# Results divided in one product and added by GpSimd, normalizations tile by tile, and scores for the maxima two a step: a decoder layer on one core

## The chip, the cores and the metric

The kernel runs on one core of a Trainium2 chip. The metric is the time of one execution on the device in microseconds (us), the median of several runs. The engines are TensorE (PE in the rows; PEld is its weight load), VectorE (DVE), ScalarE (ACT), GpSimd (POOL) and SyncE (SP), which issues most transfers. They run their own instruction streams in order and meet only at semaphores.

## The reference, cut to what matters

A decoder layer on x of 4 x 512 tokens by 512 features: causal self-attention, cross-attention to a context, and a mixture of experts, each behind a layer norm and added to x. The change lies in the cross-attention and in the layer norms computed beside it.

```python
x = x + attn(layernorm(x), w_qkv, w_proj)            # 16 heads of 128
x = x + xattn(layernorm(x), ctx_512, ctx_512)
x = x + ffn(layernorm(x), ...)                       # 8 experts, 2 a token, and a shared one

def xattn(q, k, v):      # 32 query heads, 8 key/value heads, D = 16, S = 512
    scores = einsum('bkgsd,bktd->bkgst', qh, kh) / 4
    weights = softmax(scores, axis=-1)
    out = einsum('bkgst,bktd->bkgsd', weights, vh)

def layernorm(x, eps=1e-5):
    return (x - mean(x)) / sqrt(var(x) + eps)
```

## The kernel before, in words

The residual x lies in SBUF all the time, in `res` (16 tiles of 128 tokens by 512). Self-attention runs to 954 us of the profile, cross-attention from there to 1462 us, the experts to the end.

Cross-attention works through 32 items, one for each batch b (0 to 3) and key/value head kv (0 to 7), and two more short rounds; item m is 8b + kv. Batch 0 and batch 3 are written out, batches 1 and 2 are two turns of one loop on every engine (`over_items`). In the program of an item, `cross_steps` lists what TensorE and the others do in eight steps. Three items overlap in it: the scores of the next item for its row maxima ("s", 16 a item, numbered S0 to S15 below, line 1084), the transposed scores of this item ("st", line 1095, followed by the exponential on ScalarE), the weights times the values of the last item ("pv", line 1106, in every odd step), and turns of 128 x 128 tiles on TensorE ("t", line 149): of keys ("k"), of queries ("q"), of queries with their maxima put in ("m"), and of the result of the item two before ("o", in step 4).

- VectorE takes the maximum of each score tile (line 1520). The scores use two banks of PSUM in turn, so score number u waits until the maximum of score u - 2 is taken (`s_xmax`, line 1083).
- When the turned result of an item is there, in step 4 behind S9, VectorE takes the reciprocals of the softmax sums (line 1595), multiplies the four tiles of the result by them in four products (line 1597), and adds the result to `res` (line 1603). The next turn on TensorE into the same bank waits for that add (`s_to`).
- GpSimd splits the normalized tokens `xn` into the queries of the item three ahead (`build_queries`, lines 778 to 783), adds up values (`build_values`), and puts the maxima into the queries, by pairs of heads (`put_maxima`, lines 790 to 797). TensorE's "m" turns wait for these. In item kv = 5 it first waits for all four tiles of the next batch's `xn`, then builds those queries, then the keys of the next batch (`build_keys`, lines 766 and 770), and only then puts in the first pair of maxima, for the "m" turn of step 6.
- The layer norm of the next batch is done at the start of an item, in one piece each, ahead of that item's maxima on VectorE: `moments` (four bn_stats, four bn_aggr, some small operations) at kv = 1, `roots` at kv = 2, `queries` (four products that write `xn`) at kv = 5. In batch 3, the moments for the experts' norm of batches 0 to 2 come at kv = 3, 4, 5, and the roots at kv = 4, 5, 6. The power between moments and roots is GpSimd's (line 735 or 839).

Of the kernel before, what the change touches and what calls it, by code (L numbers as in the profile page):

```python
# [6 lines left out]
P = 128  # L7
# [144 lines left out]
def moments(eng, count, src, st, first, n, s_var):  # L152

    tiles = slice(first, first + n)
    for t in range(n):
        ready = count.mark(eng.bn_stats(st["stats"][:, first + t, :], src[:, t, :]))  # L156
    eng.wait_ge(count.sem, ready)
# [20 lines left out]
RESULT_MARKS = 1 + TOK_TILES  # L178
# [8 lines left out]
VW = 32  # L187


def cross_steps(kv, m_left):  # L190
# [7 lines left out]
    for k in range(8):  # L198
        units = [("s", next(s_units)) for _ in range(1 if k % 2 else 3)] if m_left >= 1 else []
        if k % 2 == 0:  # L200
            ops += units[0:1]
            units = units[1:]
        if m_left >= 0:
            ops.append(("st", k))
        ops += units[0:1]
        if k in turns and (m_left >= turns[k][2] if turns[k][0] != "o" else kv >= 2):
            ops.append(("t",) + turns[k])
        ops += units[1:]
        if kv >= 1 and m_left >= -1 and k % 2:
            ops.append(("pv", k // 2))  # L210
    return ops


TA_START, TA_ITEM = 7, 5

# [152 lines left out]
def build(nc, x, ctx_in, w_qkv_t, w_proj_t, gate_t, w1_t, w2_t, w3_t, kinds, out):  # L368
# [11 lines left out]
    with ExitStack() as whole:  # L380
# [57 lines left out]
        s_ta = sem("s_ta")  # L438
        s_to = sem("s_to")
# [88 lines left out]
        xrec = sbb("xrec", [P, TOK_TILES, XG])  # L528
        xo = sbb("xo", [P, TOK_TILES, XG, XD])
# [187 lines left out]
        def _(pool):  # L717
# [90 lines left out]

            def cross(b, first, last):
                for kv in range(KV):  # L810
# [7 lines left out]
                    if kv == 1 and not last:  # L818
                        power_next(b)
# [26 lines left out]
            cross(BATCH - 1, False, True)  # L846

# [46 lines left out]
        def _(pe):  # L894
# [143 lines left out]
            def cross(b, kv, steps):  # L1038
# [7 lines left out]
                for op in steps:  # L1046
                    if op[0] == "t":
                        kind, which, off = op[1:]
                        if before_is_result:
                            pe.wait_ge(s_to, m - 1 if kind != "o" else m - 2)  # L1050
# [47 lines left out]
                    else:  # L1098
# [344 lines left out]
        def _(dve):  # L1443
# [66 lines left out]

            def queries(b):

                for t in range(TOK_TILES):
                    dve.tensor_scalar(xn[:, t, :], res_b[:, b, t, :], mv[:, t, 0:1], rstd[:, t:t + 1],
                                      ALU.subtract, ALU.mult).then_inc(s_xn2, 1)
# [53 lines left out]
            def cross(b, kv, steps):  # L1569
# [4 lines left out]
                if isinstance(b, int) and b == BATCH - 1:  # L1574

                    if 4 <= kv < 7:
                        roots(dve, count, norm, (kv - 4) * TOK_TILES, TOK_TILES, s_pow, 2 * BATCH + kv - 3)
                    if 3 <= kv < 6:
                        moments(dve, count, res_b[:, kv - 3], norm, (kv - 3) * TOK_TILES, TOK_TILES, s_var)
                if not (isinstance(b, int) and b >= BATCH - 1):  # L1580
                    if kv == 1:
                        moments(dve, count, res_b[:, b + 1], norm, 0, TOK_TILES, s_var)
                    if kv == 2:
                        roots(dve, count, norm, 0, TOK_TILES, s_pow, BATCH + 2 + b)
                    if kv == KV - 3:
                        dve.wait_ge(s_xq, KV * TOK_TILES * b + KV * TOK_TILES)
                        queries(b + 1)
                for op in steps:
                    if op[0] == "s":
                        maximum(m + 1, (kv + 1) % 2, op[1], XS)  # L1590
                    elif op[:2] == ("t", "o"):
# [236 lines left out]
```

## Time and profile before

| | us |
|---|---|
| median of 3 runs | 2003.03 (2002.97 to 2003.96) |
| profiled execution, its own time | 2004.67 |
| profiled execution, span in the trace | 2002.9 |
| TensorE busy in the span | 1867.5 (93%) |
| VectorE busy | 1087.9 (54%) |
| ScalarE busy | 970.2 (48%) |
| GpSimd busy | 262.9 (13%) |
| mean granted clock of TensorE | 0.971 of full speed |

Busy time of TensorE is modelled from the starts of pipelined matmuls; what counts in the rows is when a matmul starts and what it had waited for. A row of the timeline with `x4` merges four instructions that ran back to back, and its time covers all four.

### The profile page before, as it was taken

What the parts mean: (1) busy time and instruction counts of PE and PEld (TensorE: products, weight loads), DVE (VectorE), ACT (ScalarE), POOL (GpSimd) and SP (SyncE); (2) the same over time, 40 slices, a digit from 0 to 9 for tenths busy, and PEclk for the clock granted to TensorE, in tenths of its full rate; (3) what the DMA queues carried; (4) which work ended last, traced back from release to release, by engine and by line L of the source; (5) the groups of instructions that cost most, each with busy time, mean ns of one, the idle gap of its engine ahead of it and who ended that gap; (6) DMA issues with size and microseconds to landing.
All of it is one profiled execution on the core that took longest, in us unless ns stands there. A gap on an engine that the chain in (4) does not pass through costs nothing. (4 is left out here: it accounts for less than half of the span.)

```text
span 2002.9 us, 28767 instructions
## 1 busy us (share of the span) xinstructions
PE 1867.5 (93%) x9769; PEld 1316.1 (66%) x9769; DVE 1087.9 (54%) x2253; ACT 970.2 (48%) x1789; POOL 262.9 (13%) x751
## 2 busy tenths in 40 slices
PE   6999989998999989988899998998989599999998
PEld 5677667776677667765444443443379499999997
DVE  7433433342433433454777777778754126776756
ACT  3443434343433433333677776776742015666651
POOL 1000000000000000051242242433001400000015
PEclk9999989999899999999999998999989799999999
DMA  3000010000000000000000060000011318878756
GB/s 137 32 1 1 22 33 1 1 2 22 32 1 1 22 0 1 1 11 0 1 6 1 1 242 13 0 0 1 1 46 38 142 37 278 282 272 285 270 178 213
DMA packets 73393, 131.64 MB, mean 66 GB/s; under 512 B 4512, under 2 KB 35232, under 8 KB 73248
## 3 DMA queue, kind: packets, MB, share of 16 engines
q1 hardware_dynamic: 68128, 113.01, 16.4%
q0 software_dynamic: 5120, 16.78, 2.5%
q8 instruction: 80, 1.31, 0.3%
q14 instruction: 65, 0.53, 0.1%
HBM read 96.75 MB, written 33.03 MB: 65 GB/s over the span
## 5 line engine op out<-in xcount | busy, mean ns | idle before, releaser
L1520 DVE TENSOR_REDUCE xmax<-ps 128x1 f32<-128x512 f32 x512 | 329.2, 686 | 110.9 <-PE ps L1084 104.1
L1349 ACT ACTIVATE xp<-ps 128x1024 f32<-128x1024 f32 x256 | 262.9, 1029 | 140.1 <-PE ps L1095 136.2
L1282 ACT ACTIVATE probs<-ps,nmax 128x128 f32<-128x128 f32 (+3 forms) x256 | 135.5, 529 | 313.9 <-DVE nmax L1496 313.0
L1496 DVE TENSOR_REDUCE nmax<-ps 128x1 f32<-128x128 f32 (+3 forms) x256 | 126.2, 493 | 237.7 <-PE ps L926 232.1
L1084 PE MATMUL ps<-k,q 64*128 64x512 f32 x496 | 217.9, 479 | 34.3 <-DVE xmax L1520 34.3
L1084 PEld LDWEIGHTS ps<-k,q 64*128 64x128 f32 x496 | 86.0, 186 | 202.1 <-DVE xmax L1520 163.9
L926 PE MATMUL ps<-k_t,q_t 128*128 128x128 f32 (+3 forms) x512 | 201.1, 476 | 0.0
L1095 PE MATMUL ps<-q3m,k 64*128 64x512 f32 x512 | 181.9, 452 | 0.0
L149 PE MATMUL ps<-ident,probs 128*128 128x128 f32 x704 | 127.6, 286 | 42.1 <-DVE probs L1504 28.2
L1005 PE MATMUL ps<-pt,v_s 128*128 128x128 f32 (+3 forms) x512 | 161.0, 460 | 2.7 <-ACT pt L1320 2.5
L149 PEld LDWEIGHTS ps<-ident,probs 128*128 128x128 f32 x704 | 89.5, 145 | 100.6 <-issue 66.5
L1106 PE MATMUL ps<-xp,vx 128*32 128x512 f32 x1024 | 140.5, 623 | 1.4 <-issue 1.3
L143 PE MATMUL ps<-xh,wh 128*128 128x512 f32 x384 | 129.6, 459 | 2.1 <-DVE wl L1476 2.1
L143 PE MATMUL ps<-w12h,x_h 128*128 128x352 f32 x568 | 121.9, 336 | 10.0 <-issue 8.7
L1005 PEld LDWEIGHTS ps<-pt,v_s 128*128 128x128 f32 x512 | 88.4, 201 | 58.6 <-ACT pt L1320 32.4
L735 POOL TENSOR_TENSOR rstd<-ve,half 128x4 f32<-128x4 f32 x9 | 11.2, 1247 | 876.7 <-DVE ve L162 876.7
L1549 DVE TENSOR_TENSOR al<-ps,ah 128x512 fp32r<-128x512 f32 x64 | 44.3, 692 | 142.2 <-ACT ah L1325 142.2
L143 PE MATMUL ps<-w12h,x_l 128*128 128x352 f32 x568 | 115.9, 325 | 2.7 <-issue 1.8
L143 PE MATMUL ps<-w12l,x_h 128*128 128x352 f32 x568 | 115.1, 324 | 0.0
L1554 DVE TENSOR_TENSOR res<-ps,res 128x512 f32<-128x512 f32 x64 | 44.3, 692 | 123.2 <-PE ps L143 123.2
L1504 DVE TENSOR_SCALAR probs<-probs,rinv 128x128 f32<-128x128 f32 (+3 forms) x256 | 105.7, 413 | 9.1
L1320 ACT COPY pt<-ps 128x128 f32<-128x128 f32 (+3 forms) x256 | 108.8, 425 | 2.8 <-PE ps L149 2.7
(179 smaller groups left out, 3351.1 us busy)
## 6 DMA issues: line engine op xcount, KB each, us to landing
w_raw<-in_w_t SPq DMA_DIRECT2D x56, 704.0 KB, 5.9
w_raw<-in_w_t SPq DMA_DIRECT2D x28, 768.0 KB, 5.9
rows_x<-w_raw SPq DMA_DIRECT2D x1, 9984.0 KB, 30.0
mixed<-rows_x SPq DMA_DIRECT2D x39, 256.0 KB, 4.4
rows_y<-y_s SPq DMA_DIRECT2D x39, 256.0 KB, 5.4
w_raw<-in_w_qkv_t SPq DMA_DIRECT2D x4, 1536.0 KB, 6.6
res<-in_x SPq DMA_DIRECT2D x4, 1024.0 KB, 12.3
w_raw<-in_w_proj_t SPq DMA_DIRECT2D x4, 1024.0 KB, 5.1
```

Source lines behind the costliest of these rows:

```text
L143: last = pe.matmul(dst, lhs, rhs, start=(n == 0), stop=(n == len(pairs) - 1))
L149: return pe.matmul(dst, src, ident, start=True, stop=True, is_transpose=True)
L926: pe.matmul(ps[:, S_BANK + u % 2, 0:w], q_t[:, b % 2, h, i * P:w], k_t[:, b % 2, 0:w], start=False, stop=True, skip_group_check=True).then ...
L1005: ins = pe.matmul(ps[:, O_BANK + h % 2, j * P:], v_s[:, b % 2, j, :], pt[:, j, j * P:], start=(j == TOK_TILES - 1), stop=True, skip_group_ ...
L1084: pe.matmul(ps[:, XS + op[1] % 2, :], q3[half_of(h), (kv + 1) % 2, h // 2, i * P:(i + 1) * P], k3[half_of(h), (kv + 1) % 4, :], start=True ...
L1095: ins = pe.matmul(ps[:, XST + 2 * (t % 2) + h % 2, :], k3[half_of(h), kv % 4, t * P:(t + 1) * P], q3m[half_of(h), pair, :], start=True, st ...
L1106: ins = pe.matmul(ps[VW * h:VW * (h + 1), XO, :], vx[:, before % 4, j, :], xp[:, (kv - 1) % 2, h, j, :], start=(j == 0), stop=(j == TOK_TI ...
L1282: act.activation(probs[:, u % 4, 0:w], ps[:, S_BANK + u % 2, 0:w], ACT.Exp, bias=nmax[:, u % 4:u % 4 + 1], accum_out=rsum[:, u % 4:u % 4 + ...
L1320: act.copy(pt[:, 0:i + 1, i * P:(i + 1) * P], ps[:, T_BANK + (1 + t) % 2, 0:(i + 1) * P].rearrange("p (j n) -> p j n", n=P))\
L1349: act.activation(xp[:, kv % 2, 2 * pair:2 * pair + 2, t, :], ps[:, XST + 2 * (t % 2):XST + 2 * (t % 2) + 2, :], ACT.Exp, scale=X_SCALE).th ...
L1496: dve.tensor_reduce(nmax[:, u % 4:u % 4 + 1], ps[:, S_BANK + u % 2, 0:w], AX_X, ALU.max, negate=True).then_inc(s_max, 1)
L1520: dve.tensor_reduce(xmax[:, slot, i, h:h + 1], ps[:, bank + u % 2, :], AX_X, ALU.max, negate=True).then_inc(s_xmax, 1)
```

## The change

The result takes one product of 128 x 256 in place of four of 128 x 64 (`divide`), and writes it to one of two buffers; GpSimd then adds it to `res` (`add_result`), between the two `put_maxima` of the item. TensorE's next turn into the bank waits for the product (`s_od`) and not for the add. The product is made at the end of the step, or behind the next maximum.

Moments, roots and queries are cut up and placed behind steps ("end" in the list, `norm_piece`): one bn_stats behind steps 1, 3, 5 and 7 of item kv = 1, what gathers them behind step 0 of kv = 2, the roots behind step 0 of kv = 4, and the four tiles of `xn` behind steps 5 and 7 of kv = 4 and steps 0 and 1 of kv = 5. In batch 3 the same pieces come at kv = 2 to 4 (stats), 3 to 5 (gathered) and 5 to 7 (roots). Each step has two scores, where even steps had three and odd steps one.

```diff
@@ cross_steps @@
-        units = [("s", next(s_units)) for _ in range(1 if k % 2 else 3)] if m_left >= 1 else []
-        if k % 2 == 0:
-            ops += units[0:1]
-            units = units[1:]
+        units = [("s", next(s_units)) for _ in range(2)] if m_left >= 1 else []
+        ops += units[0:1]
         if m_left >= 0:
             ops.append(("st", k))
-        ops += units[0:1]
+        ops += units[1:]
         if k in turns and (m_left >= turns[k][2] if turns[k][0] != "o" else kv >= 2):
             ops.append(("t",) + turns[k])
-        ops += units[1:]
         if kv >= 1 and m_left >= -1 and k % 2:
             ops.append(("pv", k // 2))
+        ops.append(("end", k))
...
+QUERY_AT = [(4, 5), (4, 7), (5, 0), (5, 1)]
@@ GpSimd @@
+            def add_result(b, kv, m):
+                pool.wait_ge(s_od, m - 1)
+                at = ((kv - 2) % KV) * XG * XD
+                dst = res[:, :, :].rearrange("p (b t) c -> p b t c", b=BATCH)[:, b - (kv < 2), :, at:at + XG * XD]
+                pool.tensor_tensor(dst, xo[:, kv % 2].rearrange("p (t h) d -> p t (h d)", t=TOK_TILES), dst, ALU.add)\
+                    .then_inc(s_to, 1)
...
-                    if kv == 1 and not last:
+                    if kv == 3 and not last:
                         power_next(b)
...
-                    if last and 3 <= kv < 6:
-                        power(kv - 3, 2 * BATCH + kv - 2)
+                    if last and 4 <= kv < 7:
+                        power(kv - 4, 2 * BATCH + kv - 3)
                     if not (last and kv == KV - 1):
                         put_maxima((kv + 1) % 4, 0, 16 * m + 24, 2 * m + 3)
+                    if not (first and kv < 2):
+                        add_result(b, kv, m)
+                    if not (last and kv == KV - 1):
                         put_maxima((kv + 1) % 4, 1, 16 * m + 32, 2 * m + 4)
@@ TensorE @@
-                            pe.wait_ge(s_to, m - 1 if kind != "o" else m - 2)
+                            pe.wait_ge(s_od, m - 1 if kind != "o" else m - 2)
@@ VectorE @@
+                def norm_piece(k):
+                    if isinstance(b, int) and b == BATCH:
+                        return
+                    if final:
+                        if 2 <= kv < 5 and k % 2:
+                            if k == 1:
+                                dve.wait_ge(s_to, KV * (kv - 1))
+                            tile_moments(dve, count, res_b[:, kv - 2], norm, (kv - 2) * TOK_TILES, k // 2)
+                        if 3 <= kv < 6 and k == 0:
+                            gather_moments(dve, count, norm, (kv - 3) * TOK_TILES, TOK_TILES, s_var)
+                        if 5 <= kv and k == 0:
+                            roots(dve, count, norm, (kv - 5) * TOK_TILES, TOK_TILES, s_pow, 2 * BATCH + kv - 4)
+                        return
+                    if kv == 1 and k % 2:
+                        tile_moments(dve, count, res_b[:, b + 1], norm, 0, k // 2)
+                    if (kv, k) == (2, 0):
+                        gather_moments(dve, count, norm, 0, TOK_TILES, s_var)
+                    if (kv, k) == (4, 0):
+                        roots(dve, count, norm, 0, TOK_TILES, s_pow, BATCH + 2 + b)
+                    if (kv, k) in QUERY_AT:
+                        t = QUERY_AT.index((kv, k))
+                        if t == 0:
+                            dve.wait_ge(s_xq, KV * TOK_TILES * b + KV * TOK_TILES)
+                        query(b + 1, t)
+                def divide(ready):
+                    dve.wait_ge(s_dve, ready)
+                    if not (isinstance(m, int) and m < 4):
+                        dve.wait_ge(s_to, m - 3)
+                    o = ps[:, XT, :].rearrange("p (g d) -> p g d", d=VW)
+                    dve.tensor_tensor(xo[:, kv % 2], o[:, :, 0:XD],
+                                      xrec[:, :].unsqueeze(2).to_broadcast([P, TOK_TILES * XG, XD]), ALU.mult)\
+                        .then_inc(s_od, 1)
                 for op in steps:
                     if op[0] == "s":
                         maximum(m + 1, (kv + 1) % 2, op[1], XS)
+                    if op[0] in ("s", "end") and pending is not None:
+                        divide(pending)
+                        pending = None
+                    if op[0] == "end":
+                        norm_piece(op[1])
+                    if op[:2] == ("t", "o"):
                         dve.wait_ge(s_ot, m - 1)
-                        o = ps[:, XT, :].rearrange("p (t h d) -> p t h d", t=TOK_TILES, h=XG)
-                        count.seal(dve, dve.reciprocal(xrec[:, :, :], o[:, :, :, XD]))
-                        for t in range(TOK_TILES):
-                            ready = count.mark(dve.tensor_tensor(
-                                xo[:, t], o[:, t, :, 0:XD],
-                                xrec[:, t, :].unsqueeze(2).to_broadcast([P, XG, XD]), ALU.mult))
-                        dve.wait_ge(s_dve, ready)
-                        at = ((kv - 2) % KV) * XG * XD
-                        dst = res_b[:, b - (kv < 2), :, at:at + XG * XD]
-                        dve.tensor_tensor(dst, xo[:, :, :, :].rearrange("p t h d -> p t (h d)"), dst, ALU.add)\
-                            .then_inc(s_to, 1)
+                        o = ps[:, XT, :].rearrange("p (g d) -> p g d", d=VW)
+                        pending = count.mark(dve.reciprocal(xrec[:, :], o[:, :, XD]))
```

On VectorE, from the end of item 3 to item 5 of batch 0, there stands before (xmax is a maximum of a score tile, xrec the reciprocals, xo the divided result, xn a tile of normalized tokens):

```order
L1520 TENSOR_REDUCE xmax<-ps 128x1 x16
L1595 RECIPROCAL xrec<-ps 128x16
L1597 TENSOR_TENSOR xo<-ps,xrec 128x64 x4
L1603 TENSOR_TENSOR res<-xo,res 128x4x64
L1520 TENSOR_REDUCE xmax<-ps 128x1 x6
L1514 TENSOR_SCALAR xn<-res,mv,rstd 128x512 x4
L1520 TENSOR_REDUCE xmax<-ps 128x1 x10
L1595 RECIPROCAL xrec<-ps 128x16
L1597 TENSOR_TENSOR xo<-ps,xrec 128x64 x4
L1603 TENSOR_TENSOR res<-xo,res 128x4x64
```

and at the same place of the changed kernel:

```order
L1654 RECIPROCAL xrec<-ps 128x16
L1639 TENSOR_TENSOR xo<-ps,xrec 128x256
L1548 TENSOR_REDUCE xmax<-ps 128x1 x2
L1537 TENSOR_SCALAR xn<-res,mv,rstd 128x512
L1548 TENSOR_REDUCE xmax<-ps 128x1 x4
L1537 TENSOR_SCALAR xn<-res,mv,rstd 128x512
L1548 TENSOR_REDUCE xmax<-ps 128x1 x2
L1537 TENSOR_SCALAR xn<-res,mv,rstd 128x512
L1548 TENSOR_REDUCE xmax<-ps 128x1 x2
L1537 TENSOR_SCALAR xn<-res,mv,rstd 128x512
L1548 TENSOR_REDUCE xmax<-ps 128x1 x6
L1654 RECIPROCAL xrec<-ps 128x16
```

The add has left VectorE, the product is one, and the fourth tile of xn now stands behind the fourth maximum of item 5, where all four stood ahead of its first.

Also on VectorE, the moments in item 1, before (all of item 0's and item 1's maxima around one block):

```order
L1520 TENSOR_REDUCE xmax<-ps 128x1 x16
L156 BN_STATS stats<-res 128x6 x4
L158 MEMSET nt 128x4
L160 BN_AGGR mv<-stats 128x2 x4
L162 TENSOR_SCALAR ve<-mv 128x4
L1520 TENSOR_REDUCE xmax<-ps 128x1 x16
```

and now (the first row has the 16 maxima of item 0 and four of item 1):

```order
L1548 TENSOR_REDUCE xmax<-ps 128x1 x20
L160 BN_STATS stats<-res 128x6
L1548 TENSOR_REDUCE xmax<-ps 128x1 x4
L160 BN_STATS stats<-res 128x6
L1548 TENSOR_REDUCE xmax<-ps 128x1 x4
L160 BN_STATS stats<-res 128x6
L1548 TENSOR_REDUCE xmax<-ps 128x1 x4
L160 BN_STATS stats<-res 128x6
L1548 TENSOR_REDUCE xmax<-ps 128x1 x2
L167 MEMSET nt 128x4
L169 BN_AGGR mv<-stats 128x2 x4
L171 TENSOR_SCALAR ve<-mv 128x4
```

Each bn_stats stands behind four maxima, and the rest of the block behind two more.

On GpSimd, item 5 of batch 0, behind the queries (vx is build_values, kc build_keys, xq<-xmax put_maxima), before:

```order
L787 TENSOR_TENSOR vx<-kc 128x4x16 [waits s_xpv]
L766 TENSOR_TENSOR kc<-ctx_s,ones 128x16x16 [waits s_ctx,s_vx,s_kt]
L766 TENSOR_TENSOR kc<-ctx_s,ones 128x16x16 x7
L770 TENSOR_TENSOR kc<-ctx_s,kc 128x16x16 [waits s_pc]
L770 TENSOR_TENSOR kc<-ctx_s,kc 128x16x16 x3
L756 TENSOR_TENSOR xq<-xmax,ones 128x4x2 [waits s_xmax]
L796 TENSOR_TENSOR xq<-xmax,xq 128x4x2 [waits s_pm]
L756 TENSOR_TENSOR xq<-xmax,ones 128x4x2 [waits s_xmax]
L796 TENSOR_TENSOR xq<-xmax,xq 128x4x2 [waits s_pm]
```

and now:

```order
L798 TENSOR_TENSOR vx<-kc 128x4x16 [waits s_xpv]
L777 TENSOR_TENSOR kc<-ctx_s,ones 128x16x16 [waits s_ctx,s_vx,s_kt]
L777 TENSOR_TENSOR kc<-ctx_s,ones 128x16x16 x7
L781 TENSOR_TENSOR kc<-ctx_s,kc 128x16x16 [waits s_pc]
L781 TENSOR_TENSOR kc<-ctx_s,kc 128x16x16 x3
L767 TENSOR_TENSOR xq<-xmax,ones 128x4x2 [waits s_xmax]
L807 TENSOR_TENSOR xq<-xmax,xq 128x4x2 [waits s_pm]
L826 TENSOR_TENSOR res<-xo,res 128x4x64 [waits s_od]
L767 TENSOR_TENSOR xq<-xmax,ones 128x4x2 [waits s_xmax]
L807 TENSOR_TENSOR xq<-xmax,xq 128x4x2 [waits s_pm]
```

Only the add of the result has come in. TensorE's whole list of instructions is the same in both kernels, row by row, since a step of three scores and one of one, laid end to end, give the same order as two steps of two.

## Rows read from the trace of the kernel before

**Rows 1.** The page's first line: span and instructions.

```profile
span 2002.9 us, 28767 instructions
```

**Rows 2.** Waits, 950 to 1465 us: engine, line, waited for, us, times, longest.

```profile
PEld ps L1084 <- DVE xmax L1520: 163.9, 299, 3.3
```

**Rows 3.** Timeline of TensorE, item 25: start, us, what, idle before.

```profile
1356.44 1.06 PE L1106 MATMUL ps<-xp,vx 128*32 128x512 f32 x8
1357.88 0.49 PE L1084 MATMUL ps<-k,q 64*128 64x512 f32 x1 [0.38 <-DVE xmax L1520]
...
1358.91 0.65 PE L149 MATMUL ps<-ident,xq 128*128 128x128 f32 x4
```

**Rows 4.** Timeline of VectorE, items 25 to 27.

```profile
1354.66 1.29 DVE L1520 TENSOR_REDUCE xmax<-ps 128x1 f32<-128x512 f32 x2 [0.73 <-PE ps L1084]
1355.87 0.25 DVE L1595 RECIPROCAL xrec<-ps 128x16 f32<-128x16 f32 x1
1356.15 0.62 DVE L1597 TENSOR_TENSOR xo<-ps,xrec 128x64 f32<-128x64 f32 x4
1356.80 0.43 DVE L1603 TENSOR_TENSOR res<-xo,res 128x256 f32<-128x256 f32 x1
1357.15 2.56 DVE L1520 TENSOR_REDUCE xmax<-ps 128x1 f32<-128x512 f32 x4
...
1362.36 2.56 DVE L1520 TENSOR_REDUCE xmax<-ps 128x1 f32<-128x512 f32 x4 [1.04 <-PE ps L1084]
1366.27 2.57 DVE L1520 TENSOR_REDUCE xmax<-ps 128x1 f32<-128x512 f32 x4 [1.35 <-PE ps L1084]
...
1376.14 2.46 DVE L156 BATCH_NORM_STATS2 stats<-res 128x6 f32<-128x512 f32 x4
```

**Rows 5.** Timeline of ScalarE: the copy that closes items 16 to 18.

```profile
1221.88 0.59 ACT L1357 COPY o_t<-ps 128x512 f32<-128x512 f32 x1 [0.19 <-PE ps L1106]
...
1240.21 0.59 ACT L1357 COPY o_t<-ps 128x512 f32<-128x512 f32 x1 [0.20 <-PE ps L1106]
...
1255.30 0.59 ACT L1357 COPY o_t<-ps 128x512 f32<-128x512 f32 x1 [0.19 <-PE ps L1106]
```

**Rows 6.** The same copy, closing items 25 to 29.

```profile
1361.96 0.59 ACT L1357 COPY o_t<-ps 128x512 f32<-128x512 f32 x1 [0.19 <-PE ps L1106]
...
1376.87 0.59 ACT L1357 COPY o_t<-ps 128x512 f32<-128x512 f32 x1 [0.19 <-PE ps L1106]
...
1393.68 0.59 ACT L1357 COPY o_t<-ps 128x512 f32<-128x512 f32 x1 [0.20 <-PE ps L1106]
...
1412.53 0.59 ACT L1357 COPY o_t<-ps 128x512 f32<-128x512 f32 x1 [0.19 <-PE ps L1106]
...
1431.38 0.59 ACT L1357 COPY o_t<-ps 128x512 f32<-128x512 f32 x1 [0.19 <-PE ps L1106]
```

**Rows 7.** Timeline of TensorE: first scores of items 1 and 2.

```profile
966.11 0.46 PE L1084 MATMUL ps<-k,q 64*128 64x512 f32 x1
...
985.33 0.49 PE L1084 MATMUL ps<-k,q 64*128 64x512 f32 x1
```

**Rows 8.** Windows, item 17: us, busy time of each engine, then the granted clock.

```profile
1226.00:1228.00 2.00, 2.00 (x9) 0.92 (x12) 0.93 (x2) 1.56 (x2) 0.40 (x2) 0.50 0.00 0
```

**Rows 9.** Timelines of VectorE, TensorE and GpSimd, item 21.

```profile
1284.76 1.91 DVE L1514 TENSOR_SCALAR xn<-res,mv,rstd 128x512 f32 x4
...
1285.34 0.50 PE L1084 MATMUL ps<-k,q 64*128 64x512 f32 x1
...
1286.83 2.05 POOL L756 TENSOR_TENSOR xq<-xn,ones 128x64 fp32r<-128x64 f32 x8 [1.00 <-DVE xn L1514]
...
1295.41 3.00 POOL L770 TENSOR_TENSOR kc<-ctx_s,kc 128x256 fp32r<-128x256 f32 x4
...
1298.65 0.22 POOL L796 TENSOR_TENSOR xq<-xmax,xq 128x8 fp32r<-128x8 f32 x1
...
1298.92 0.66 PE L149 MATMUL ps<-ident,xq 128*128 128x128 f32 x4 [0.73 <-POOL xq L796]
```

More of the change, by code:

```diff
@@ L152, in moments, with tile_moments, gather_moments @@
 def moments(eng, count, src, st, first, n, s_var):
+    for t in range(n):
+        tile_moments(eng, count, src, st, first, t)
+    gather_moments(eng, count, st, first, n, s_var)
+def tile_moments(eng, count, src, st, first, t):
+    count.mark(eng.bn_stats(st["stats"][:, first + t, :], src[:, t, :]))
+def gather_moments(eng, count, st, first, n, s_var):
     tiles = slice(first, first + n)
-    for t in range(n):
-        ready = count.mark(eng.bn_stats(st["stats"][:, first + t, :], src[:, t, :]))
-    eng.wait_ge(count.sem, ready)
+    eng.wait_ge(count.sem, count.start + count.n)
     count.mark(eng.memset(st["nt"][:, tiles], 0.0))
@@ L176 @@
 NORM_MARKS = 2 * TOK_TILES + 5
-RESULT_MARKS = 1 + TOK_TILES
+RESULT_MARKS = 1
 KV, XG, XD = 8, 4, 16
@@ L438, in build @@
         s_ta = sem("s_ta")
+        s_od = sem("s_od")
         s_to = sem("s_to")
@@ L527, in build @@
         xmax = sbb("xmax", [P, 2, TOK_TILES, XG])
-        xrec = sbb("xrec", [P, TOK_TILES, XG])
-        xo = sbb("xo", [P, TOK_TILES, XG, XD])
+        xrec = sbb("xrec", [P, TOK_TILES * XG])
+        xo = sbb("xo", [P, 2, TOK_TILES * XG, XD])
         pb.close()
@@ L846, in _ @@
             cross(BATCH - 1, False, True)
+            for kv in range(2):
+                add_result(BATCH, kv, KV * BATCH + kv)
             pool.wait_ge(s_to, ITEMS)
@@ L1097, in cross @@
                         ins.then_inc(s_st, 1)
-                    else:
+                    elif op[0] == "pv":
                         j, before = op[1], (kv - 1) % KV
@@ L1509, in _, with query @@
             res_b = res[:, :, :].rearrange("p (b t) c -> p b t c", b=BATCH)
+            def query(b, t):
+                dve.tensor_scalar(xn[:, t, :], res_b[:, b, t, :], mv[:, t, 0:1], rstd[:, t:t + 1],
+                                  ALU.subtract, ALU.mult).then_inc(s_xn2, 1)
             def queries(b):
                 for t in range(TOK_TILES):
-                    dve.tensor_scalar(xn[:, t, :], res_b[:, b, t, :], mv[:, t, 0:1], rstd[:, t:t + 1],
-                                      ALU.subtract, ALU.mult).then_inc(s_xn2, 1)
+                    query(b, t)
             def maximum(m, slot, u, bank):
@@ L1573, in cross @@
                 count = counts[-1]
[L1574 to L1583, printed above, removed]
-                        roots(dve, count, norm, 0, TOK_TILES, s_pow, BATCH + 2 + b)
-                    if kv == KV - 3:
-                        dve.wait_ge(s_xq, KV * TOK_TILES * b + KV * TOK_TILES)
-                        queries(b + 1)
+                final = isinstance(b, int) and b == BATCH - 1
@@ L1590, in cross @@
                         maximum(m + 1, (kv + 1) % 2, op[1], XS)
[L1591 to L1604 removed]
+                    if op[0] in ("s", "end") and pending is not None:
+                        divide(pending)
+                        pending = None
+                    if op[0] == "end":
+                        norm_piece(op[1])
+                    if op[:2] == ("t", "o"):
+                        dve.wait_ge(s_ot, m - 1)
+                        o = ps[:, XT, :].rearrange("p (g d) -> p g d", d=VW)
+                        pending = count.mark(dve.reciprocal(xrec[:, :], o[:, :, XD]))
             over_items(cross)(dve)
```

## The prediction, made before the changed kernel ran

> **What bounds the kernel now.** I read the page first. The change touches only cross-attention, so I asked for the waits of that stretch. Neither TensorE nor VectorE fills it: TensorE's scores wait for VectorE's maxima, 163.9 us in 299 waits [rows 2], and the maxima wait for scores in between. So the stretch is a ping-pong over two banks, and what counts is where VectorE does something else while TensorE wants a bank. The reader is to see three places of that kind in the timelines.
>
> First, the result, in nearly every item. The reciprocal starts at 1355.87, the maximum that TensorE needs next at 1357.15, so VectorE is away for 1.28 us [rows 4]. TensorE's product with the values ends at 1357.50 (1356.44 + 1.06), it stands for 0.38 us until the next score at 1357.88, the score behind that is late too, and the turn starts at 1358.91 [rows 3]. An ordinary item lasts 14.91 us in written-out code (1361.96 to 1376.87) [rows 6] and 15.09 us in the loop (1240.21 to 1255.30) [rows 5].
>
> Second, the blocks of the layer norm. Item 27 begins with four bn_stats of 2.46 us together and their small operations [rows 4] and lasts 16.81 us, 1.90 over the ordinary; items 28 and 29, with moments and roots in one block, last 18.85 us each, 3.94 over [rows 6]. Item 17 has the moments alone and lasts 18.33 us, 3.24 over [rows 5], since TensorE's granted clock was 0.50 there, which is 1.2 GHz where 2.4 is full [rows 8]: it fell after TensorE had stood waiting for the block. Against the 1.90 of item 27 the clock cost 1.34 us. Item 1 lasts from 966.11 to 985.33, 19.22 us [rows 7]; it has no result to divide, so I take 14.4 for it without the block (14.91 less the 0.5 or so that the result costs), and it is 4.8 over.
>
> Third, GpSimd in items 5, 13 and 21. In item 21 it starts the queries at 1286.83, when the fourth tile of xn has ended (1284.76 + 1.91 = 1286.67), works without a break through queries, values and keys, and puts in the first maxima at 1298.65; TensorE's turn follows at 1298.92 after standing 0.73 us [rows 9]. GpSimd is already the last one there.
>
> **The change part by part.** The order of TensorE's instructions is the same, so "two a step" by itself is worth nothing; it only names the places behind which VectorE's pieces go.
>
> The result: reciprocal 0.28 us start to start (1355.87 to 1356.15), then one product of 256 elements a partition. No row has that product. The add of the same 256 elements took 0.43, and 0.35 start to start (1356.80 to 1357.15); the four products took 0.62 [rows 4]. I take the 0.35, since it has the same number of elements in one instruction, with the 0.62 as the upper end and the 0.25 that the reciprocals of 16 elements took as the lower. The next maximum then starts 0.28 + 0.03 + 0.35 = 0.66 us after the reciprocal, not 1.28, a gain of 0.62; the loop has one more wait with a computed value, so I take 0.60 for all. Does TensorE get it? The next score had 0.38 us to gain and the one behind it waits for the second maximum, so that and the turn move by all 0.6. The ends are 0.35 (product 0.62) and 0.7 (product 0.25). Items that have it whole: 2, 3, 6, 7, 8, 10, 11, 14, 15, 16, 18, 19, 22, 23, 24, 25. 16 x 0.60 = **9.6 us**.
>
> The moments: a bn_stats costs 2.46/4 = 0.61 us. Behind steps 1, 3 and 7 VectorE stands idle 1.35, 0.73 and 1.04 us for the next score [rows 4], which covers it; if that cover went, each would cost up to 0.61. Behind step 5 there is no idle time, and it takes just what the shorter result gave, so items 9, 17, 26, 27 and 28 gain nothing from the result. Gathering and roots stand behind the second maximum, where TensorE needs the third only after a product with values; up to about 1 us hides. So the blocks' prices come back: items 1, 9, 17, 27, 28, 29: 4.8 + 1.9 + 3.24 + 1.90 + 3.94 + 3.94 = **19.7 us**, with item 9 taken like item 27.
>
> Small change: in items 4, 12 and 20 a tile of xn (1.91/4 = 0.48 us [rows 9]) stands behind step 5, leaving 0.12 of the 0.60 each; in items 29 and 30 the roots with what stands beside them are longer than what hides them, I keep 0.3 of the 0.60 in each. Together **1.0 us**.
>
> The queries, which is the part against: all four tiles of xn stood ahead of the item's first maximum, and now the last stands behind its fourth. In item 21 GpSimd started 1.49 us after the item's first score (1285.34 to 1286.83) [rows 9]. Now: the score takes 0.50, two maxima 1.28 (2.56/4 each [rows 4]), a tile 0.48, two maxima 1.28, the last tile 0.48, and 0.16 to hand over as before, 4.18 us. GpSimd starts 2.7 us later, nothing on it is shorter (the add stands behind the maxima it is late with), and it was already late. TensorE reaches its turn earlier and stands there: the turn was 13.58 us into the item (1298.92 - 1285.34), is at 16.3, and without the wait would be at about 11.6. So the three items get 3 x 2.7 = 8.1 us longer, and TensorE stands some 4 us in each. After such a stand the clock fell in item 17; I add its 1.34 us in two of the three, since the rows don't show a fall behind every stand (item 27 had the same block as item 17 and kept its clock, by its length). **-10.8 us**. Two queues pass on this delay: behind GpSimd's first maxima stand the add, the second maxima and the next queries, but the second maxima wait for S15 anyway, so nothing more is late.
>
> GpSimd's add: the nearest row is L770, two inputs from SBUF and 128 x 256, 3.00/4 = 0.75 us [rows 9], against 0.43 on VectorE. It stands between the two pairs of maxima, and the second pair waits for S15, over 6 us behind the result, so the add is hidden there. The Trainium skill (GPSIMD Engine Reference, section 3, Performance versus the Vector engine) says elementwise work is about twice as slow on GpSimd and gives "use DVE for elementwise" as the rule; the rows agree on the ratio. The add is waited for once, the last one before the experts: 0.75 - 0.43 and a hand-over, **-0.35 us**.
>
> Sum: 9.6 + 19.7 + 1.0 - 10.8 - 0.35 = 19.2 us. The profiled span of 2002.9 [rows 1] lies within 0.2 of the median 2003.03 (that execution's own time was 2004.67), so I set the sum against the median: **1984 us**.
>
> **The rivals.**
> - GpSimd is in time after all (the wait for xn is not what starts it, or the turn finds the maxima ready). Then the -10.8 goes and the three items gain up to 0.6 each as well: 2003 - 31 = 1972 to 1973. Against it: the row of 0.73 us shows GpSimd late already. 1 in 10.
> - The product costs what the four did, or the stands in items 5, 13 and 21 cost twice the clock price because they are twice as long as item 17's: 16 x 0.25 = 4 us, or 3 x 1.34 = 4 us less gain. 1988. Nothing in the rows excludes either. 15 in 100.
> - The shorter result doesn't reach TensorE, because the second of the two scores waits for something else there (the copies of ScalarE, the turn's bank): 9.6 and 1 go; or VectorE and TensorE do wait for GpSimd's slower add in every item, 30 x (0.75 - 0.43) = 9.6. 1994 to 1995. The timeline names the maximum as the one waited for, and the only wait for the add, before a product, is for that of four items before, so 11 in 100. The second half of this is what the rule of the Trainium skill quoted above (GPSIMD Engine Reference, section 3) would lead one to expect.
> - Slower: TensorE's clock. The clock fell after stands of TensorE; if the new rhythm, with VectorE's pieces spread over many items, made it fall in ordinary items too, each fall would cost 1.34 us. The 19.2 us are used up after 14 falls, and it is slower by over 0.2% from 18 on. The rows show ordinary items, with stands of 0.4 us, at even length, and the spreading takes stands away. 4 in 100.
>
> **How the numbers follow.** The forecast has 60 in 100. The range of 8 in 10 goes from 1973, the first rival, to 1993: the ends of the product's price (0.35 to 0.7 us on 16 items, +4 and -2), the clock price (0 to 2 x 1.34 in three items, +5 and -3) lie inside. 0.2% is 4 us, about what a measurement of this kernel tells from no change: below 1999 is faster. All cases but the last and a part of the third lie there: faster 0.93, same 0.04, slower 0.03.
>
> **What would show it.** In the profile of the changed kernel: ordinary items 14.3 us written out and 14.5 in the loop; one product of some 0.4 us and the next maximum 0.66 us after the reciprocal; items 1, 27, 28 and 29 near 14.4 to 15, with no fall of the clock there; items 13 and 21 at 19 to 21 us, longer than before, with TensorE waiting over 4 us for GpSimd's put_maxima, and a granted clock near 0.5 behind it; GpSimd's add 0.75 us, waited for by nobody but the end. The prediction is wrong if that wait is not there, or if the ordinary items keep their length.

## The result, and the profile after

The changed kernel takes **1986.07 us** (median of 6 runs, 1977.9 to 1991.96), the kernel before 2003.49 us (median of 6, 2001.99 to 2008.4) in the same comparison: a ratio of 0.9906, 95% interval 0.9881 to 0.993. That is 17.4 us, with 19.2 forecast: faster, and inside the range. The profiled execution of the changed kernel is its slowest run (1991.96 us).

The first line of the page, which answers to [rows 1]:

```profile
span 1990.0 us, 28687 instructions
```

The waits of the stretch, which answer to [rows 2] (engine, line, waited for, us in total, times, longest): one more line of the kernel before (950 to 1465 us), then the changed kernel (950 to 1450 us):

```profile
PE ps L1084 <- DVE xmax L1520: 34.3, 44, 3.0
```

```profile
PEld ps L1109 <- DVE xmax L1548: 137.8, 330, 3.5
...
PE ps L149 <- POOL xq L807: 13.4, 3, 4.5
POOL xq L767 <- DVE xn L1537: 12.1, 3, 4.1
...
PE ps L1109 <- DVE xmax L1548: 5.1, 6, 3.2
```

The wait for the maxima fell from 163.9 to 137.8 us ahead of TensorE's weight loads, and from 34.3 us in 44 waits to 5.1 in 6 ahead of its matmuls. Between the two stands a pair of three waits each, and these are items 5, 13 and 21: GpSimd waits 12.1 us for the layer-normed tiles, and TensorE 13.4 us for GpSimd. That is the part of the prediction that spoke against the change.

VectorE and then TensorE around the result of an ordinary item (24), which answer to [rows 4] and [rows 3] (start, us, what, idle before and who ended it):

```profile
1346.98 0.25 DVE L1654 RECIPROCAL xrec<-ps 128x16 f32<-128x16 f32 x1
1347.26 0.42 DVE L1639 TENSOR_TENSOR xo<-ps,xrec 128x256 f32<-128x256 f32 x1
1347.60 1.28 DVE L1548 TENSOR_REDUCE xmax<-ps 128x1 f32<-128x512 f32 x2
```

```profile
1347.55 1.06 PE L1131 MATMUL ps<-xp,vx 128*32 128x512 f32 x8
...
1348.55 0.49 PE L1109 MATMUL ps<-k,q 64*128 64x512 f32 x1
...
1349.36 0.66 PE L149 MATMUL ps<-ident,xq 128*128 128x128 f32 x4
```

From the reciprocal to the next maximum it is 0.62 us (1346.98 to 1347.60) where it was 1.28, and one product takes 0.42. The score behind the product with values has no wait any more (it had 0.38 us), and the turn starts 1.81 us after that product's start (1347.55 to 1349.36), where it was 2.47.

ScalarE's copy closes each item, so the spacing of these rows is the length of an item. Items 1 and 2, then 4 and 5, then 20 and 21, then 27 to 29; they answer to [rows 5] and [rows 6]:

```profile
981.03 0.59 ACT L1382 COPY o_t<-ps 128x512 f32<-128x512 f32 x1 [0.37 <-PE ps L1131]
995.44 0.58 ACT L1382 COPY o_t<-ps 128x512 f32<-128x512 f32 x1 [0.36 <-PE ps L1131]
...
1024.44 0.58 ACT L1382 COPY o_t<-ps 128x512 f32<-128x512 f32 x1 [0.44 <-PE ps L1131]
1045.12 0.58 ACT L1382 COPY o_t<-ps 128x512 f32<-128x512 f32 x1 [1.07 <-PE ps L1131]
...
1274.48 0.58 ACT L1382 COPY o_t<-ps 128x512 f32<-128x512 f32 x1 [0.44 <-PE ps L1131]
1294.75 0.59 ACT L1382 COPY o_t<-ps 128x512 f32<-128x512 f32 x1 [0.62 <-PE ps L1131]
...
1382.01 0.59 ACT L1382 COPY o_t<-ps 128x512 f32<-128x512 f32 x1 [0.44 <-PE ps L1131]
1396.72 0.58 ACT L1382 COPY o_t<-ps 128x512 f32<-128x512 f32 x1 [0.44 <-PE ps L1131]
1411.14 0.59 ACT L1382 COPY o_t<-ps 128x512 f32<-128x512 f32 x1 [0.35 <-PE ps L1131]
```

Item 2 lasts 14.41 us and item 29 14.42: an ordinary item in written-out code was 14.91. Item 9 lasts 14.88, item 28 14.71 (it was 18.85), item 5 20.68 and item 21 20.27 (before: 17.83 and 16.50). The last copy of all comes at 1438.39, and came at 1459.17 before: cross-attention ends 20.8 us earlier. It also began 0.35 us later (its first score at 955.24, 954.89 before), so the stretch itself is 21.1 us shorter.

GpSimd and TensorE in item 21, which answer to [rows 9]:

```profile
1278.43 2.04 POOL L767 TENSOR_TENSOR xq<-xn,ones 128x64 fp32r<-128x64 f32 x8 [4.05 <-DVE xn L1537]
...
1290.01 0.22 POOL L807 TENSOR_TENSOR xq<-xmax,xq 128x8 fp32r<-128x8 f32 x1
1290.18 0.73 POOL L826 TENSOR_TENSOR res<-xo,res 128x256 f32 x1
```

```profile
1274.34 0.49 PE L1109 MATMUL ps<-k,q 64*128 64x512 f32 x1
...
1290.29 1.02 PE L149 MATMUL ps<-ident,xq 128*128 128x128 f32 x4 [4.46 <-POOL xq L807]
```

GpSimd starts 4.09 us into the item (1274.34 to 1278.43, was 1.49) and then works without a break up to its maxima at 1290.01; TensorE stands 4.46 us for them. Windows from within that stand to behind it (us, then busy time of PE, PEld, DVE, ACT and POOL, the granted clock, DMA):

```profile
1288.00:1290.00 2.00, 0.00 (x0) 0.00 (x0) 0.00 (x0) 0.00 (x0) 1.94 (x4) 1.00 0.00 0
1290.00:1292.00 2.00, 1.72 (x8) 1.12 (x8) 0.00 (x0) 0.58 (x1) 0.90 (x2) 0.61 0.00 0
1292.00:1294.00 2.00, 2.00 (x12) 0.92 (x12) 1.29 (x2) 1.48 (x2) 0.49 (x3) 0.54 0.00 0
```

In the first window only GpSimd works. After it TensorE comes back at a granted clock of 0.61 and 0.54, near its lower level of 1.2 GHz, and the four transposes of the turn take 1.02 us, not 0.66. In item 17, where [rows 8] showed 0.50 before, the clock is now full:

```profile
1226.00:1228.00 2.00, 1.99 (x16) 0.90 (x8) 2.00 (x5) 1.01 (x2) 0.57 (x1) 1.00 0.00 0
```

Last, the profiled span is only 12.9 us shorter (2002.9 to 1990.0), 7.9 less than cross-attention gained. TensorE's last transposes of fn start at 1971.96 in the kernel before and at 1953.43 after, so 18.5 us were left then; between cross-attention and that point 2.3 had gone, which I didn't follow to one wait. The other 5.6 us went in the last three expert steps. First the kernel before, then the changed one, TensorE:

```profile
1978.65 0.91 PE L143 MATMUL ps<-w12h,x_h 128*128 128x352 f32 x4 [1.05 <-DVE x_l L1618]
1979.40 0.80 PE L143 MATMUL ps<-w12l,x_h 128*128 128x352 f32 x4
...
1998.08 0.85 PE L1223 MATMUL ps<-w3h,hl 128*128 128x512 f32 x3
```

```profile
1957.00 0.32 PE L143 MATMUL ps<-w12h,x_l 128*128 128x352 f32 x1 [0.83 <-issue]
...
1964.44 1.54 PE L143 MATMUL ps<-w12h,x_h 128*128 128x352 f32 x4 [2.28 <-DVE x_l L1668]
1965.78 1.38 PE L143 MATMUL ps<-w12l,x_h 128*128 128x352 f32 x4
...
1985.15 0.87 PE L1248 MATMUL ps<-w3h,hl 128*128 128x512 f32 x3
```

The lead is 18.5 us at the transposes, 14.2 at the first pair (1978.65 to 1964.44) and 12.9 at the end. In between TensorE stood with nothing that the profile shows (0.83), waited 2.28 us where it had waited 1.05, and then ran its products at 1.38 us for four, not 0.80. The diff touches nothing there. Whether it belongs to the change or to one execution, the profile can't say; the sixth experiment answers it.

### The profile page after: what moved, and what is told of

The parts are those of the page before. It is cut to its first block and busy times, and to the rows that moved or that the text cites. A ratio compares the mean times of both kernels' runs of the same rounds, so it can differ in the third digit from the quotient of the medians.

```text
span 1990.0 us, 28687 instructions
## 1 busy us (share of the span) xinstructions
PE 1869.1 (94%) x9769; PEld 1321.3 (66%) x9769; DVE 1066.1 (54%) x2125; ACT 966.2 (49%) x1789; POOL 283.9 (14%) x783
## 5 line engine op out<-in xcount | busy, mean ns | idle before, releaser
L1109 PEld LDWEIGHTS ps<-k,q 64*128 64x128 f32 x496 | 85.5, 185 | 170.9 <-DVE xmax L1548 137.8
```

What stands on the lines that cost most here:

```text
L1109: pe.matmul(ps[:, XS + op[1] % 2, :], q3[half_of(h), (kv + 1) % 2, h // 2, i * P:(i + 1) * P], k3[half_of(h), (kv + 1) % 4, :], start=True ...
```

## The experiments

Experiments 1 to 4 ran in one comparison on one chip, 5 to 7 in another on another. The kernel before took 1972.85 us there (1971.81 to 1975.54, 10 runs) and 1974.08 (1971.58 to 1976.37, 9 runs), so only differences within a comparison are read.

**1. The queries earlier.** All four tiles of xn go behind odd steps of item 4 (12, 20), so GpSimd has them when it comes.

```diff
-QUERY_AT = [(4, 5), (4, 7), (5, 0), (5, 1)]
+QUERY_AT = [(4, 1), (4, 3), (4, 5), (4, 7)]
```

> The changed kernel with the four tiles of xn behind steps 1, 3, 5 and 7 of item kv = 4 in place of steps 5, 7 of kv = 4 and 0, 1 of kv = 5. Theory (the late fourth tile is what starts GpSimd late in items 5, 13 and 21): GpSimd starts the queries within 0.3 us of the item's first score in place of 4.1, its first maxima are put in 4 us earlier, TensorE waits for them 0.3 to 0.8 us in place of 4.5, the clock does not fall there, and the three items last about 15.1 us in place of 20.3 to 20.9: some 16 us less than the changed kernel, about 1968 us. Rival (GpSimd is late because its keys take 7.7 us whenever it starts, or because of something other than xn): the three items stay above 18 us and the time within 5 us of the changed kernel's 1985.

Measured: 1935.2 us (1934.97 to 1936.72), ratio 0.981 [0.9797, 0.9824], 37.6 us under the kernel before. Items 5, 13 and 21 last 14.74, 14.78 and 14.77 us. GpSimd, then TensorE:

```profile
1260.89 2.05 POOL L767 TENSOR_TENSOR xq<-xn,ones 128x64 fp32r<-128x64 f32 x8
```

```profile
1272.75 0.66 PE L149 MATMUL ps<-ident,xq 128*128 128x128 f32 x4 [0.37 <-POOL xq L807]
```

GpSimd waits for nothing ahead of the queries, and TensorE stands 0.37 us, not 4.46; the four transposes take 0.66 us again. The three items take 44.29 us together, 17.6 less than in the first profile of the changed kernel (61.88), and this kernel's gain is 17.4 us over the one that experiment 6 finds for the changed kernel (37.6 less 20.2). So the late last tiles of xn are the cause of the long items, and the clock's price goes with the stand. Against the items of experiment 6 (63.04 us) it is 18.8 less, and item 16, at the loop's end, takes 1.8 of it back here (20.11 us against 18.30; last section).

**2. The same, and GpSimd's keys in two halves.** The first maxima stand between the halves of build_keys, so GpSimd's chain ahead of them is shorter by the 2.8 us of the second.

```diff
 # GpSimd, item 5, 13, 21; the QUERY_AT of experiment 1
-                        build_keys(b + 1)
+                        build_keys(b + 1, (0,))
...
                         put_maxima((kv + 1) % 4, 0, 16 * m + 24, 2 * m + 3)
+                    if kv == KV - 3 and not last:
+                        build_keys(b + 1, (1,))
```

> As e1, and GpSimd puts in the first pair of maxima between the two halves of build_keys (after the eight products, before the four subtractions). Theory: GpSimd's first maxima are ready before TensorE's turn, no wait is left in items 5, 13 and 21, they last 14.4 to 14.6 us; another 1 to 2 us less than e1, about 1966.5 us. Rival (the next item's turn of keys now waits for the second half): the waits move by one item and e2 is no faster than e1, or slower by up to 2 us.

Measured: 1932.4 us (1930.98 to 1935.05), ratio 0.9794 [0.978, 0.9807]: the fastest kernel of the study, 40.4 us under the kernel before, where the changed kernel is 20.2 (experiment 6). Items 5, 13 and 21 last 14.44, 14.50 and 14.51 us, like any other, and no turn of maxima waits for GpSimd. The three items give 0.84 us of the 2.8 by which it is faster than experiment 1, and in the profiles item 16 is 1.22 shorter (18.89 and 20.11); the intervals of the two kernels overlap, so only the first part is shown to come from the edit. The turn of keys in the next item, which the rival had wait, doesn't: items 6, 14 and 22 last 14.41 to 14.51 us.

**3. The result part alone.** One product and GpSimd's add as in the change, the blocks of the layer norm where they were before.

```diff
-                    if kv == 1 and k % 2:
-                        tile_moments(dve, count, res_b[:, b + 1], norm, 0, k // 2)
...
+                    if kv == 1:
+                        moments(dve, count, res_b[:, b + 1], norm, 0, TOK_TILES, s_var)
```

> The result part alone: one product, add by GpSimd, norm blocks at the start of items as before. Theory: every item with a result but 5, 13 and 21 is 0.5 to 0.6 us shorter than before, 26 of them, and the blocks cost what they did: 13 to 16 us faster than before, 1988 us. Rival (the shorter result only pays where a piece of the norm takes its place, or GpSimd's add slows its maxima): under 5 us faster.

Measured: 1958.29 us (1954.22 to 1959.77), ratio 0.9926 [0.9913, 0.994], 14.6 us. Ordinary items last 14.42 and 14.50 us as in the changed kernel. The block still costs, but less than it did: item 28 lasts 17.04 us, 2.62 over the ordinary, where the excess was 3.94. VectorE at the start of item 28:

```profile
1376.86 0.15 DVE L179 TENSOR_TENSOR nt<-rstd 128x4 f32<-128x4 f32 x1
...
1377.82 2.47 DVE L160 BATCH_NORM_STATS2 stats<-res 128x6 f32<-128x512 f32 x4
...
1380.82 2.56 DVE L1548 TENSOR_REDUCE xmax<-ps 128x1 f32<-128x512 f32 x4
```

VectorE is away from TensorE's maxima for 3.96 us (1376.86 to 1380.82), and it was away for as long before, 3.94 (1392.95 to 1396.89). What differs is TensorE's granted clock behind the block. A window that begins some 3 us after the block's end, in the kernel before, then in this one:

```profile
1400.00:1402.00 2.00, 2.00 (x12) 0.51 (x4) 0.15 (x1) 0.00 (x0) 0.00 (x0) 0.50 0.04 8
```

```profile
1384.00:1386.00 2.00, 2.00 (x15) 1.01 (x11) 1.31 (x3) 1.06 (x2) 0.00 (x0) 1.00 0.03 8
```

So 1.3 us of the 3.94 were the clock (18.85 - 17.04, less 0.49 for the result), as in item 17. Behind the six blocks it fell in items 1, 17, 28 and 29 in the profile before and in items 1, 9 and 17 in this one. How long TensorE had stood doesn't decide it alone: here the clock fell after stands of 1.80 and 1.81 us (items 9 and 17) and stayed full after 2.61 and 2.49 (items 28 and 29). Item 9 is longer here than before (17.80 against 16.93), since the clock had stayed full there before.

**4. The norm part alone.** The pieces behind the steps as in the change; four products and VectorE's add as before.

```diff
-                    dve.tensor_tensor(xo[:, kv % 2], o[:, :, 0:XD],
-                                      xrec[:, :].unsqueeze(2).to_broadcast([P, TOK_TILES * XG, XD]), ALU.mult)\
-                        .then_inc(s_od, 1)
+                    for t in range(TOK_TILES):
+                        ready = count.mark(dve.tensor_tensor(x4[:, t], o[:, t, :, 0:XD],
+                                                             r[:, t, :].unsqueeze(2).to_broadcast([P, XG, XD]), ALU.mult))
+                    dve.wait_ge(s_dve, ready)
...
+                    dve.tensor_tensor(dst, xo[:, kv % 2].rearrange("p (t h) d -> p t (h d)", t=TOK_TILES), dst, ALU.add)\
```

> The norm part alone: pieces behind steps as in the changed kernel, the result in four products and an add on VectorE as before. Theory: the blocks give back 19.7 us, items 5, 13 and 21 lose about 11, and the pieces behind step 5, which now find no room, cost 0.5 each in eight items, 4 us: about 5 us faster than before, 1998 us. Together with e3 that makes the whole change (-15 and -5). Rival (the parts help each other, the sum is not the whole): e4 slower than before.

Measured: 1964.57 us (1964.28 to 1970.73), ratio 0.9963 [0.995, 0.9975], 8.3 us. Items 28 and 29 last 15.37 and 14.91 us, items 5, 13 and 21 21.11, 21.07 and 21.25. So the pieces gain at the blocks and lose at the queries, with the result as it was, and each piece behind step 5 costs what was expected (15.37 against 14.91). Some 5 us were expected, and 4.0 of the 8.3 are item 16 alone, 16.02 us where it was 20.02: a stand at the loop's end was shorter in this kernel (last section). Leaving item 16 out (it gained 0.5 in experiment 3 and 1.7 in experiment 6), the parts gave 14.1 and 4.3 us, 18.4 together, and the whole change 18.5: they add up. Item 16 is read from one execution of each kernel and the 95% intervals of the gains are 2.5 to 3 us to either side, so this is additivity within a few microseconds.

**5. One product, the add on VectorE.** The changed kernel with the add back on VectorE behind the product.

```diff
-                    if not (first and kv < 2):
-                        add_result(b, kv, m)
...
+                    dve.wait_ge(s_dve, ready)
...
+                    dve.tensor_tensor(dst, xo[:, kv % 2].rearrange("p (t h) d -> p t (h d)", t=TOK_TILES), dst, ALU.add)\
+                        .then_inc(s_to, 1)
```

> The changed kernel with the add on VectorE behind the one product, not on GpSimd. Theory (of the 0.63 us an item that VectorE gives back, the one product is 0.28 and the missing add 0.35): the next maximum starts 0.28 later than in the changed kernel at least, 1.00 us behind the reciprocal in place of 0.62; ordinary items last 14.8 us in place of 14.4 to 14.5, the whole 8 to 9 us more than e6. Rival (moving the add is worth nothing since VectorE has room): equal to e6 within 2 us.

Measured: 1963.34 us (1959.02 to 1963.61), ratio 0.9941 [0.9927, 0.9954], 9.4 us over the changed kernel in the same comparison. Ordinary items last 14.72 and 14.90 us. VectorE:

```profile
1368.11 0.25 DVE L1652 RECIPROCAL xrec<-ps 128x16 f32<-128x16 f32 x1
1368.40 0.42 DVE L1632 TENSOR_TENSOR xo<-ps,xrec 128x256 f32<-128x256 f32 x1
1368.86 0.42 DVE L1638 TENSOR_TENSOR res<-xo,res 128x256 f32<-128x256 f32 x1
1369.20 1.28 DVE L1544 TENSOR_REDUCE xmax<-ps 128x1 f32<-128x512 f32 x2
```

The next maximum starts 1.09 us after the reciprocal: 0.62 with the add on GpSimd, 1.28 in the kernel before. So of the 0.66 us that the result part takes from VectorE, 0.47 come from moving the add and 0.19 from the one product; of the item's 0.49 us in written-out code 0.30 and 0.19.

**6. The changed kernel again.** The same code as the change, in the later comparison (so no edit to show).

> The changed kernel once more, beside the kernels of this call. Theory: the 16.6 us between it and e1 and the sum of e3 and e4 hold on this chip: 1.0% to 1.2% faster than before, 19 to 23 us; cross-attention ends 20 to 21 us earlier than before, with items 5, 13 and 21 at 20 to 21 us. What differs from run to run lies behind cross-attention: the gathers and scatters of the experts. Rival (cross-attention itself varies): its items differ from the first profile by more than 2 us in all.

Measured: 1953.93 us (1950.6 to 1958.58), ratio 0.9898 [0.9882, 0.9913], 20.2 us under the kernel before. Its items 5, 13 and 21 last 20.92, 21.06 and 21.06 us. In its last three expert steps the four products take 0.80 to 0.89 us and none takes 1.38, so the loss there in the first profile doesn't come with the change each time. The expectation on cross-attention was missed, and its rival came about: the last closing copy comes at 1441.57, 17.6 us earlier than in the kernel before (whose only profile is of the first comparison) and not 20 to 21. Of the 3.2 us against the first profile, 2.2 lie ahead of the first closing copy, in item 0 and the start of item 1, where the granted clock is 0.50 from 963 to 970 us:

```profile
964.00:966.00 2.00, 2.00 (x10) 1.23 (x9) 1.29 (x2) 1.29 (x2) 0.00 (x0) 0.50 0.00 0
```

TensorE had stood for no more than 0.40 us at a time since 955. Experiments 2 and 7 show a fall at the same place, the first profiles and the other experiments don't; what brings it isn't shown. The remaining 1 us is mostly the clock behind the stands of items 5, 13 and 21, which reached into items 6 and 14 here (14.90 and 14.83 us), less 0.8 at item 16.

**7. The last tile of xn later still.** One step more.

```diff
-QUERY_AT = [(4, 5), (4, 7), (5, 0), (5, 1)]
+QUERY_AT = [(4, 5), (4, 7), (5, 0), (5, 2)]
```

> The changed kernel with the fourth tile of xn behind step 2 of item kv = 5 in place of step 1. Theory (every microsecond that the last tile is later makes the item as much longer): GpSimd starts 2.2 to 2.4 us later, TensorE stands 6.7 us in place of 4.5, items 5, 13 and 21 last 22.5 to 23.2 us, about 7 us more than e6 in all. Rival (the stand is set by the clock or by the keys): under 3 us more.

Measured: 1959.91 us (1957.78 to 1963.04), ratio 0.9927 [0.9914, 0.9941], 6.0 us over the changed kernel. Items 5, 13 and 21 last 22.40, 23.40 and 23.39 us. GpSimd, then TensorE, in item 21:

```profile
1287.02 2.05 POOL L767 TENSOR_TENSOR xq<-xn,ones 128x64 fp32r<-128x64 f32 x8 [6.40 <-DVE xn L1537]
```

```profile
1298.87 1.12 PE L149 MATMUL ps<-ident,xq 128*128 128x128 f32 x4 [6.80 <-POOL xq L807]
```

GpSimd waits 2.35 us longer than in the changed kernel (4.05 to 6.40), TensorE 2.34 longer (4.46 to 6.80), and the item against experiment 6 2.33 longer (21.06 to 23.39). One late tile is passed on whole through two engines. The clock's price didn't grow with the stand: item 21 is 2.1 us longer than an ordinary item and the wait explain (23.39 - 14.50 - 6.80), as it is in experiment 6 (21.06 - 14.50 - 4.47). In item 5 it was less here, 1.3 us (22.40 - 14.42 - 6.70), and in experiment 6 it was 2.5 with what ran over into item 6.

## Why the prediction was right

The mechanism held, and the number too: 17.4 us measured, 19.2 forecast. In the profiles the stretch itself gained 21.1 us, 21.0 with the add at the end. By its terms:

- **The result**, 9.6 us. Measured 9.25 over the same 16 items. The step on VectorE was right almost to the digit (0.66 forecast, 0.62 measured, the product 0.42 long and 0.34 start to start). In the loop an item gained 0.59 us, in written-out code 0.49: the turn comes 0.66 us sooner in written-out code, and 0.17 go again later in the item, which I didn't trace. I had reckoned the same 0.60 for both. Item 16 gained 0.93, and the 0.3 over the others aren't VectorE's stand at the loop's end, which was longer (3.98 us before, 4.32 after); TensorE's clock was below full for some 3.5 us there, and for some 6.5 before.
- **The moments and roots**, 19.7 us. Measured 20.9: item 1 4.75 (by its first scores, 966.43 to 980.90 after), item 9 2.05, item 17 3.46, items 27 to 29 2.10, 4.14 and 4.43. I had let the piece behind step 5 take all that the shorter result gave. It takes 0.29 to 0.38 us (14.71 against 14.42, 14.88 against 14.50), so each item with such a piece kept 0.2 to 0.3. The clock stayed full in item 17, as said. But I had read all of items 28 and 29's 3.94 us as the block's length, and item 1's 4.8 too, and the clock into item 17 alone. It had fallen in all four (experiment 3), and had stayed full behind the same block in items 9 and 27. The sum was right, because the pieces took the stands away and the falls with them. But at 1.3 us a fall about 5 us of the 19.7 are the clock's, an estimate, and which blocks pay it differs between the profiles.
- **Small change**, 1.0 us. Measured 2.0: the tile of xn behind step 5 cost about 0.15 us and not the whole of its 0.48, so items 4, 12 and 20 kept 0.35 to 0.45 and not 0.12; items 26 and 30 gave 0.2 and 0.5. Same error as above: a piece of 0.5 to 0.6 us there costs less than its length, presumably since VectorE then has less idle time behind the next step.
- **The queries**, -10.8 us. Measured -11.1: 2.85, 4.44 and 3.77. GpSimd's start was forecast 4.18 us into the item and came at 4.09, the turn 16.3 and came at 15.95 (1290.29 - 1274.34), the stand some 4 us and was 4.4 to 4.5. Experiments 1 and 7 show this from both sides: the tile earlier and the stand is gone, later and it grows by as much. The clock's part was forecast as 1.34 us in two items of three. It fell in all three; by the items' lengths over wait and ordinary item it cost 1.8, 1.9 and 1.3 us (20.68 - 14.42 - 4.44, 20.93 - 14.50 - 4.49, 20.27 - 14.50 - 4.46). But in item 5 it had fallen in the kernel before too (granted clock 0.60 from 1044 to 1046), so the new falls are two, and there the sum was right for a reason that it didn't have.
- **GpSimd's add**, -0.35 us. It takes 0.73 us (0.75 forecast), and of all 32 only the last is waited for, by the layer norm and a weight load ahead of the experts:

```profile
1441.34 1.92 DVE L1486 TENSOR_SCALAR fn_all<-res,mv,rstd 128x512 f32<-128x512 f32 x4 [0.84 <-POOL res L826]
```

The step from the last closing copy to this row is 2.95 us (1438.39 to 1441.34), was 2.80 (1459.17 to 1461.97): 0.15 us more and not 0.35, since the saved products pay for a part. The twice-as-slow rule of the Trainium skill (GPSIMD Engine Reference, section 3) comes out as 1.7 here, 0.73 us against 0.43, and by it the add should have stayed on VectorE; experiment 5 puts it there and loses 9.4 us, since VectorE is the engine that TensorE waits for and GpSimd has idle time. The row decides, not the rule.

None of the rivals came about. GpSimd was not in time; the shorter result did reach TensorE; the clock fell in no ordinary item of the first profile (it did in item 0 of experiment 6, at a cost of 2.2 us). The second rival's clock price, twice 1.34 us in each of the three, wasn't reached there: 1.3 to 1.9. It nearly was in experiment 6, 2.1 to 2.5 with what ran over into the next items. The sum was 1.8 us too small in cross-attention by the profiles, and the experts' stretch, in which executions differ by some us, took 7.9 off again in the profiled execution. That the medians came as near as 17.4 (20.2 in the other comparison) is in part luck: the interval of the ratio goes from 14 to 24 us.

## What to carry to other kernels

When an engine takes a block apart and spreads it, ask of each piece who starts on the last one: moments could go behind any step for nothing or for 0.3 to 0.4 us an item, but the four tiles of xn start a chain of 11.6 us on GpSimd (1278.43 to 1290.01), and their delay came out whole at TensorE, with 1.3 to 2.5 us of clock on top. Price work by the engine that is waited for: an add of 0.73 us on an idle engine is cheaper than one of 0.43 on the engine that everybody wants. And look at the granted clock behind each wait before you call an item's extra length the work's: 1.3 of 3.94 us here were the clock. With that one piece placed by whom it starts (experiments 1 and 2), the same change gains twice as much: 2.1% against 1.0%.

## What was unexpected of the hardware

**VectorE stands at the end of the loop.** At the one place where the loop's body starts again (item 16), VectorE stands for microseconds while the profile names nothing that it waits for. The chain of waits of the changed kernel, then of experiment 4 (start, us):

```profile
1196.07 4.32 issue
```

```profile
1202.52 1.90 issue
```

It was 3.98 us in the kernel before, 4.86 in experiment 1, 4.05 in experiment 2, 2.47 in experiment 5. TensorE stands 3.21 us behind it in the changed kernel, its clock is 0.50 in the window from 1202 to 1204, and item 16 lasts 19.09 us there, against 16.02 in experiment 4, which is most of that experiment's surplus. In experiment 4 the clock stayed full there. No run here varied the loop, so the cause stays open.

**TensorE's instructions come slowly in some executions.** The same code ran 32 us faster in the later comparison (1986.07 and 1953.93). Most of that is one place, the stretch in which GpSimd issues its indirect DMAs of rows_x: from 1500 to 1600 us TensorE transposes hid for 11 tiles in the first profile and for 15 in experiment 6, and 15 in the next 100 us in both, so the four tiles are some 27 us, an estimate. Two windows of the changed kernel's first profile, then of experiment 6:

```profile
1540.00:1560.00 20.00, 5.91 (x16) 4.24 (x16) 1.08 (x2) 0.48 (x1) 15.34 (x16) 0.58 0.55 210
1560.00:1580.00 20.00, 13.94 (x57) 11.90 (x58) 4.15 (x7) 2.33 (x5) 2.88 (x3) 0.66 0.22 80
```

```profile
1540.00:1560.00 20.00, 20.00 (x119) 18.73 (x118) 4.63 (x8) 3.40 (x7) 15.13 (x17) 1.00 0.54 206
1560.00:1580.00 20.00, 20.00 (x119) 18.69 (x118) 6.01 (x10) 3.95 (x8) 4.52 (x5) 1.00 0.30 105
```

GpSimd is as busy and the DMA share as high in both (0.55 and 0.54), yet TensorE issues 16 matmuls in one and 119 in the other. Its timeline in the first shows single matmuls with gaps that the profile puts down to no other engine:

```profile
1556.49 0.37 PE L149 MATMUL ps<-ident,hid 128*96 128x128 f32 x1 [1.73 <-issue]
1559.28 0.59 PE L1248 MATMUL ps<-w3h,hh 128*128 128x512 f32 x1 [2.42 <-issue]
```

The kernel before has the same gap in its first profile: from 1540 to 1600 TensorE is busy 37.41 of 60 us at a clock of 0.80. So ratios within a comparison (0.9906 and 0.9898) agree while the times don't. (The kernel before, too, was 29 us faster in the later comparisons, 1972.85 and 1974.08 where it took 2003.49.) Whether it hangs on the chip or on the moment, and what holds the instructions back, no run here tells.
